# Roll layer by two images: VectorE's step reordered, the residual added by TensorE and moved by ScalarE; attention's output bias added in the embedding

## The chip, the cores and the metric

The kernel runs on one core of a Trainium2 chip. The metric is the device time of one execution in microseconds (us); lower is better. All data is float32.

## The reference, cut to what matters

32 images of 36 patches and 32 text tokens each give 68 tokens per image, 2176 tokens of 256 features, in 17 tiles of 128 tokens.

```
h = concat(patchify(x) @ W.T + b, txt)            # (32, 68, 256)
h = h + attention(layernorm(h))                   # windowed, 16 heads; ends in  out @ Wo + bo
h = h + ffn0(layernorm(h))                        # 64 experts, 8 per token, plus a shared one
h = h + roll(layernorm(h))
h = h + ffn1(layernorm(h))                        # 8 experts, 1 per token

roll(x):                                          # per image, S = 68, H = 16 heads of 16
  z = softmax((x @ W_A.T) * 16**-0.5, axis=tokens)            # (S, H)
  v = (x @ W_V.T).reshape(S, H, 16)
  out[i, h] = sum over j of  (z rolled by i, lower triangle)[h, i, j] * v[j, h]
  return out @ W_O.T + b_O
```

The kernel computes the rolled sum as a product of Fourier transforms over the tokens: transform v and z (real and imaginary part), multiply, transform back.

## The kernel before, in words

The stages follow each other with a barrier between them: `embed_and_norm` (L176), attention (`window_attention`, L342), the first mixture of experts, `roll_layer` (L1469), the second mixture. `h` is the residual stream [128, 17 tiles, 256] in SBUF, `xn` its normalised rows, `xT` these transposed.

**Embedding.** Four batches of eight images. TensorE sums the patches to columns and transposes them to tiles; VectorE copies a tile to `h`, takes its statistics, and normalises it to `xn` (L338); TensorE transposes `xn` back and ScalarE moves it to `xT` (L252). The batches have 4, 4, 4 and 5 tiles. SP loads patches, text and constants, then the attention weights wq, wk, wv and the biases bq, bk, bv, bo in this order, all on one semaphore, `attn_in`; attention waits for all seven (112).

**Attention.** Eight blocks of four images, eight steps in each. VectorE's step adds the mask (L566), takes the peak (L570) and normalises the step three before (L549, L553); in block 0 it also adds `bo` to two tiles of `h` per step (L545), and the seventeenth tile's add follows after the last block. POOL subtracts the peak (L425). The attention's own output is added to `h` in a later stage.

**Roll layer.** Sixteen groups of two images (136 tokens), in a software pipeline of 19 steps. In step i, group g1 = i-1 is on the way in, g2 = i-2 is multiplied, inverted and projected, and g3 = i-3 goes out; the order on each engine is written out by hand. On the way in, a tile of `h` gets its eight expert rows added (`combine`, L1854; POOL gathers them at L1571 into a ring of four tiles), is measured (L1861, L1862), its rstd is made on ScalarE (`root`, a logarithm and an exponential, L1763 and L1766), `scale` makes the shift on VectorE (L1869), ScalarE normalises (L1772), TensorE turns it (`turn`, L1583) and ScalarE moves it (L1778). Then come `mix_logits` (L1591: z in PSUM, moved by ScalarE at L1751), `values` (L1601, moved at L1758), and the softmax of z over the 68 tokens on [16, 2, 68]: `mix_shift` on VectorE (maximum L1874, subtraction L1875), `exp` on ScalarE (L1787), `mix_norm` on VectorE (sum L1880, reciprocal L1881, product L1882). `turn_mix` (L1616) and `forward_mix` (L1622) transform z, ScalarE moves both results (L1791, L1798). In the next step, `forward` transforms v, one product for the real part and one for the imaginary part (L1610), `multiply` makes four terms on VectorE (L1901), `invert` transforms back in 64 products (L1635), ScalarE moves the result (`move_out`, L1744), and `project` multiplies by W_O into `pr`, with b_O added by a product with the identity (L1645, L1647). One step later VectorE adds `pr` to `h` (`add_projected`, L1889), the tile is measured, normalised and turned a second time ("out"), and `choose` (L1668) makes the router logits of the last layer. SP writes the normalised tile and `h` to DRAM.

On VectorE a step is in this order before: scale in, add_projected, measure out, four multiplies, scale out, mix_shift, combine 0 to 3, mix_norm, combine 4 to 7, measure in. On TensorE: forward (both parts), turn in, mix_logits, values, turn out, invert, turn_mix, project, choose, forward_mix. On ScalarE: root in, normalise in, move turned in, root out, normalise out, move_mix, move_values, move turned out, exp, move_out, move_mix_turned, move_mix_forwarded. Steps 1, 2 and 16 have additional products without use on TensorE (`fill_logits`, `fill_values`).

Of the kernel before, what the change touches and what calls it, by code (L numbers as in the profile page):

```python
# [5 lines left out]
P = 128  # L6
D = 256
# [4 lines left out]
S = NPATCH + NTXT  # L12
# [163 lines left out]
def embed_and_norm(nc, a, k):  # L176
# [6 lines left out]
    with ExitStack() as st:  # L183
# [11 lines left out]
        (consts_in, bias_in, attn_in, txt_in, sums, moved, txt_placed, turned, placed, stated, measured, eps_set, rooted, inverted,  # L195
         normed, turned_back, turn_moved) = sems(
            nc, k, "emb", "consts_in bias_in attn_in txt_in sums moved txt_placed turned placed stated measured eps_set rooted inverted "
# [9 lines left out]
        with nc.Block() as block:  # L207

            @block.sync
            def _(sp):  # L210
# [109 lines left out]
            def _(dve):  # L320
                for i in range(NB):
# [15 lines left out]
                    for t in range(lo, hi):  # L337
                        nc.vector.tensor_scalar(xn[:, t, :], h[:, t, :], mv[:, t, 0:1], rstd[:, t:t + 1],  # L338
                                                ALU.subtract, ALU.mult).then_inc(normed, 1)


def window_attention(nc, a, k, m, aT, wo):  # L342
# [18 lines left out]
    with ExitStack() as st:  # L361
        sb = lambda n, s, d=fp32: k["sb"](f"wa_{n}", s, d, st)
        wq, wk, wv, bq, bk, bv, bo = (k["attn"][n] for n in ("wq", "wk", "wv", "bq", "bk", "bv", "bo"))
# [18 lines left out]
         peaked, shifted, exped, turn_moved, inverted, normalised, biased, ones_all) = sems(  # L382
            nc, k, "wa", "block_copied keys_spread vals_set scored masked turned weighted jobs_done "
            "jobs_moved placed peaked shifted exped turn_moved inverted normalised biased ones_all")
# [22 lines left out]
        with nc.Block() as block:  # L407
# [10 lines left out]
            def _(pool):  # L418
                nc.gpsimd.tensor_copy(xb[:, :, :], xT[:, :, 0:CB]).then_inc(block_copied, 1)
                head_of = k["const"]("head_of").unsqueeze(2).broadcast_to([P, PER, S])  # L420
                pool.wait_ge(w_in, 112)
# [35 lines left out]
            def _(pe):  # L457
# [6 lines left out]
                pe.wait_ge(w_in, 112)  # L464
# [78 lines left out]
            def _(dve):  # L543
                def add_bias(t):
                    nc.vector.tensor_tensor(h[:, t, :], h[:, t, :], bo[:, :], ALU.add).then_inc(biased, 1)  # L545

# [9 lines left out]
                def body(blk, table):  # L556
                    start = isinstance(blk, int) and blk == 0
                    for step in range(UNITS):
# [24 lines left out]
                add_bias(NT - 1)  # L583
# [4 lines left out]
            def _(act):  # L588
# [38 lines left out]
                act.wait_ge(w_in, 112)  # L627
# [841 lines left out]
def roll_layer(nc, a, k, r, wt, y_rows, shared_up, shared_down):  # L1469
# [30 lines left out]
    with ExitStack() as st:  # L1500
# [7 lines left out]
        zpeak, zsum = sb("zpeak", [H, GI]), sb("zsum", [H, GI])  # L1508
# [14 lines left out]
         z_shifted, exped, z_normed, z_turned, zt_moved, zf_done, zf_moved, v_done, v_moved, forwarded, terms,  # L1523
# [835 lines left out]
```

## Time and profile before

| what | value |
|---|---|
| three runs | 1069.63, 1071.5, 1072.02 us; median 1071.5 |
| profiled execution | 1072.1 us, its span 1070.3 us |
| mean granted TensorE clock of the span | 0.938 |
| busy over the span | TensorE 928.9 us (87%), VectorE 591.7 (55%), POOL 523.0 (49%), ScalarE 420.7 (39%) |
| roll layer | about 635 to 870 us of the span |
| steady steps of the roll layer | one is 758.12 to 769.13 us of the span |

The span goes from the first to the last instruction of one profiled execution. Shares are means over stages that have different limits, so a stage is read in the timeline of its own stretch. Names such as PE, DVE, ACT, POOL and SP are TensorE, VectorE, ScalarE, GpSimd and SyncE; L1882 is line 1882 of the kernel.

### The profile page before, as it was taken

What the parts mean: (1) busy time and instruction counts of PE and PEld (TensorE: products, weight loads), DVE (VectorE), ACT (ScalarE), POOL (GpSimd) and SP (SyncE); (2) the same over time, 40 slices, a digit from 0 to 9 for tenths busy, and PEclk for the clock granted to TensorE, in tenths of its full rate; (3) what the DMA queues carried; (4) which work ended last, traced back from release to release, by engine and by line L of the source; (5) the groups of instructions that cost most, each with busy time, mean ns of one, the idle gap of its engine ahead of it and who ended that gap; (6) DMA issues with size and microseconds to landing.
All of it is one profiled execution on the core that took longest, in us unless ns stands there. A gap on an engine that the chain in (4) does not pass through costs nothing. (4 is left out here: it accounts for less than half of the span.)

```text
span 1070.3 us, 29582 instructions
## 1 busy us (share of the span) xinstructions
PE 928.9 (87%) x10270; PEld 740.1 (69%) x10270; DVE 591.7 (55%) x1502; ACT 420.7 (39%) x1158; POOL 523.0 (49%) x714
## 2 busy tenths in 40 slices
PE   8689999987824999999999987889888945999996
PEld 6557777766823888888888876455555535888895
DVE  1678888866896677533333425687877551111111
ACT  2346676742424343343434421243433312332331
POOL 0055655620502777777677717777773002333332
PEclk9889999979968999999999999898998986999998
DMA  7010000002002988977788833354482046476650
GB/s 254 14 32 2 0 0 0 1 2 76 10 0 83 321 261 263 295 230 221 251 267 254 236 93 96 104 130 123 123 289 71 21 172 223 141 262 216 262 155 25
DMA packets 79820, 149.27 MB, mean 139 GB/s; under 512 B 18892, under 2 KB 53327, under 8 KB 75760
## 3 DMA queue, kind: packets, MB, share of 16 engines
q1 hardware_dynamic: 34768, 77.15, 21.4%
q0 software_dynamic: 17712, 47.88, 16.0%
q10 hardware_dynamic: 27248, 23.09, 6.4%
q8 instruction: 49, 0.80, 0.3%
q14 instruction: 43, 0.35, 0.1%
HBM read 200.22 MB, written 31.73 MB: 217 GB/s over the span
## 5 line engine op out<-in xcount | busy, mean ns | idle before, releaser
L1309 POOL DMA_INDIRECT x_x<-m_x_rows,x_idx x170 | 165.8, 975 | 74.6 <-issue 35.5
L1335 PE MATMUL x_pup<-x_xt,x_w 128*128 128x128 f32 (+1 forms) x2176 | 183.9, 251 | 0.0
L1335 PEld LDWEIGHTS x_pup<-x_xt,x_w 128*128 128x128 f32 (+1 forms) x2176 | 167.9, 165 | 5.8 <-issue 5.7
L1571 POOL DMA_INDIRECT rl_y<-m_y_rows,rl_idx x136 | 133.7, 983 | 45.6 <-issue 36.9
L1405 DVE TENSOR_TENSOR x_hid<-x_gate,x_pup 128x128 f32<-128x128 f32 x170 | 49.0, 288 | 148.0 <-ACT x_gate L1377 141.3
L1349 PE MATMUL x_pdown<-x_w,x_hid 128*128 128x256 f32 (+1 forms) x408 | 104.2, 389 | 0.2 <-DVE x_y L1412 0.2
L1373 ACT ACTIVATE x_xt<-x_pturn 128x256 f32<-128x256 f32 x170 | 65.2, 383 | 89.0 <-PE x_pturn L1320 86.1
L425 POOL TENSOR_TENSOR wa_probs<-wa_probs,wa_peak 68x544 f32<-68x544 f32 x64 | 70.8, 1106 | 59.5 <-DVE wa_peak L570 59.5
L2295 DVE TENSOR_TENSOR x_y<-x_pdown,x_b 128x256 f32<-128x256 f32 x21 | 8.9, 425 | 153.4 <-PE x_pdown L2251 153.4
L2281 ACT ACTIVATE x_hid<-x_pup,x_b 128x128 f32<-128x128 f32 (+1 forms) x200 | 52.7, 355 | 96.0 <-PE x_pup L2234 95.8
L1377 ACT ACTIVATE x_gate<-x_pup 128x128 f32<-128x128 f32 x170 | 47.1, 277 | 92.8 <-PE x_pup L1335 92.1
L1320 PE MATMUL x_pturn<-cst,x_x 128*128 128x128 f32 x340 | 68.0, 282 | 9.6 <-DMA x_x<-m_x_rows,x_idx 9.6
L1412 DVE COPY x_y<-x_pdown 128x256 f32<-128x256 f32 x170 | 71.3, 420 | 2.0 <-PE x_pdown L1349 0.5
L1320 PEld LDWEIGHTS x_pturn<-cst,x_x 128*128 128x128 f32 x340 | 45.3, 142 | 37.1 <-issue 13.1
L1854 DVE SCALAR_TENSOR_TENSOR h<-rl_y,m_wt,h 128x256 f32<-128x256 f32 x136 | 65.8, 484 | 3.8
L2190 POOL DMA_INDIRECT out_h<-x_y,m_ids_out x21 | 21.2, 1007 | 93.5 <-DVE x_y L2298 87.3
L618 ACT ACTIVATE wa_probs<-wa_probs 68x544 f32<-68x544 f32 x64 | 42.1, 658 | 51.7 <-POOL wa_probs L425 51.6
L1294 POOL COPY x_idx<-m_ids 128x1 uint32 (+1 forms) x170 | 37.2, 219 | 41.5 <-POOLq L902 40.5
L2234 PE MATMUL x_pup<-x_xt,late_w 128*128 128x128 f32 x384 | 48.2, 287 | 3.7 <-ACT x_xt L2271 1.9
L2234 PEld LDWEIGHTS x_pup<-x_xt,late_w 128*128 128x128 f32 x384 | 47.1, 202 | 6.2 <-issue 3.7
L1349 PEld LDWEIGHTS x_pdown<-x_w,x_hid 128*128 128x128 f32 (+1 forms) x408 | 48.1, 173 | 3.9 <-DVE x_hid L1405 0.6
L566 DVE TENSOR_TENSOR wa_probs<-wa_scores,cst 68x544 f32<-68x544 f32 x64 | 46.0, 718 | 8.1 <-PE wa_scores L521 5.8
(327 smaller groups left out, 1895.0 us busy)
## 6 DMA issues: line engine op xcount, KB each, us to landing
x_w<-in_experts SPq DMA_DIRECT2D x204, 384.0 KB
late_w<-in_w SPq DMA_DIRECT2D x28, 1024.0 KB, 12.3
m_y_rows<-x_y ACTq DMA_DIRECT2D x170, 128.0 KB
xT<-in_w SPq DMA_DIRECT2D x12, 1024.0 KB, 6.2
xn<-in_w SPq DMA_DIRECT2D x10, 1024.0 KB, 10.5
h<-in_w SPq DMA_DIRECT2D x10, 1024.0 KB, 14.6
m_x_rows<-xn SPq DMA_DIRECT2D x34, 128.0 KB, 1.8
x_x<-m_x_rows,x_idx POOLq DMA_INDIRECT x170, 4.7
```

Of the source, the lines that this page charges most:

```text
L425: nc.gpsimd.tensor_tensor(probs[:, slot4, :, :], probs[:, slot4, :, :], peak[:, slot2, :].unsqueeze(2).broadcast_to([S, HC, S]), ALU.subtr ...
L1309: nc.gpsimd.indirect_dma_start(x[:, s, :], None, x_rows, bass.IndirectOffsetOnAxis(ap=idx[:, s:s + 1], axis=0))\
L1320: mm = nc.tensor.transpose(pturn[:, bank, c * P:(c + 1) * P], x[:, s, c * P:(c + 1) * P], ident)
L1335: mm = nc.tensor.matmul(pup[rows:rows + wide, bank, m * P + side * wide:m * P + (side + 1) * wide], w[:, lane, first:first + wide], xt[:, ...
L1349: mm = nc.tensor.matmul(pdown[rows, s % 2, 0:D], hid[:, s, rows], w[:, lane, UP:W], start=True, stop=True)
L1373: nc.scalar.activation(xt[:, s, :], pturn[:, bank, 0:D], ACT.Copy).then_inc(turn_moved, 1)
L1405: nc.vector.tensor_tensor(hid[:, s, :], gate[:, s, :], pup[:, bank, P:2 * P], ALU.mult)\
L1412: nc.vector.tensor_copy(y[:, s, :], pdown[:, s % 2, 0:D]).then_inc(down_moved, 1)
L1571: nc.gpsimd.indirect_dma_start(y[:, t % YR, kk, :], None, y_rows, bass.IndirectOffsetOnAxis(ap=idx[:, n:n + 1], axis=0))\
L1854: nc.vector.scalar_tensor_tensor(h[:, t, :], y[:, t % YR, kk, :], wt[:, t, kk:kk + 1], h[:, t, :], ALU.mult, ALU.add).then_inc(added, 1)
L2234: mm = nc.tensor.matmul(pup[rows:rows + wide, s, half, to:to + wide], w1[l][:, c, first:first + wide], xt[:, s, at:at + wide], start=(c == ...
L2281: ins = nc.scalar.activation(hid[:, s, f, side * wide:(side + 1) * wide], pup[:, s, f // HB, at:at + wide], ACT.Gelu, bias=b1[:, l, f:f + 1])
```

## The change

Attention's output bias: `bo` gets a semaphore of its own (`bo_in`) and is loaded first among the attention weights; VectorE adds it to `h` in `embed_and_norm`, after each batch's normalise for the batch before, and for the last batch behind it. The adds of attention's block 0 are gone.

Roll layer: (1) `project` adds the residual tile by a product of the identity with `h`, ScalarE moves the sum from PSUM to `h` (`move_projected`), and `add_projected` is gone. (2) z is negated as it is moved, VectorE takes one minimum (`mix_least`), and ScalarE's exponential takes it as a bias with scale -1, one instruction for each image, which also gives the sum; the subtraction and the sum on VectorE are gone. (3) The order on the three engines is another one, and `forward` and `multiply` are split into their two parts.

```diff
@@ embed_and_norm, SP
+                sp.dma_start(attn["bo"][:, :], a["bo"].broadcast_to([P, D])).then_inc(bo_in, 16)
                 for name in ("wq", "wk", "wv"):
...
-                sp.dma_start(attn["bo"][:, :], a["bo"].broadcast_to([P, D])).then_inc(attn_in, 16)
@@ embed_and_norm, VectorE
+                def add_bias(i):
+                    dve.wait_ge(bo_in, 16)
+                    dve.wait_ge(normed, BATCHES[i][1])
+                    for t in range(*BATCHES[i]):
+                        nc.vector.tensor_tensor(h[:, t, :], h[:, t, :], attn["bo"][:, :], ALU.add).then_inc(residual_biased, 1)
...
+                    if i:
+                        add_bias(i - 1)
+                add_bias(NB - 1)
@@ window_attention, VectorE
-                        if start:
-                            for t in range(2 * step, 2 * step + 2):
-                                add_bias(t)
...
-                add_bias(NT - 1)
@@ roll_layer, TensorE
                         nc.tensor.matmul(pr[:, s, :], ident, late["b_o"][:, :], start=True, stop=False)
+                        nc.tensor.matmul(pr[:, s, :], ident, h[:, t, :], start=False, stop=False)
...
                     if has2:
-                        forward(g2, 0)
                         forward(g2, 1)
...
+                    if has2:
                         invert(g2)
+                    if has2 and not has1:
...
                     for t in outs:
                         turn("out", t)
...
-                    if has2 and has1:
-                        invert(g2)
                     if has1:
                         turn_mix(g1)
                     if has2 and has1:
                         project(g2)
-                    for t in outs:
-                        choose(t)
...
                     if has1:
                         forward_mix(g1)
+                        forward(g1, 0)
+                    for t in outs:
+                        choose(t)
@@ roll_layer, ScalarE
+                def move_projected(g):
+                    ts = tiles_out(g)
+                    act.wait_ge(projected, g + 1)
+                    nc.scalar.activation(h[:, ts[0]:ts[-1] + 1, :], pr[:, 0:len(ts), :], ACT.Copy).then_inc(proj_added, 1)
...
-                                         scale=float(HD) ** -0.5).then_inc(z_moved, 1)
+                                         scale=-float(HD) ** -0.5).then_inc(z_moved, 1)
...
-                    nc.scalar.activation(z[:, :, :], z[:, :, :], ACT.Exp).then_inc(exped, 1)
+                    act.wait_ge(least_found, g + 1)
+                    for b in range(GI):
+                        ins = nc.scalar.activation(z[:, b, :], z[:, b, :], ACT.Exp, bias=zleast[:, b:b + 1], scale=-1.0,
+                                                   accum_out=zsum[:, b:b + 1])
+                    ins.then_inc(exped, 1)
...
+                    if has1:
+                        move_mix(g1)
...
                     if outs:
                         root("out", outs)
+                    if has1:
+                        move_values(g1)
+                    if outs:
                         normalise("out", outs)
...
                         exp(g1)
                     if has2 and has1:
                         move_out(g2)
+                    for t in outs:
+                        move_turned("out", t)
                     if has1:
                         move_mix_turned(g1)
+                    if has2:
+                        move_projected(g2)
+                    if has1:
                         move_mix_forwarded(g1)
@@ roll_layer, VectorE
+                    nc.vector.tensor_reduce(zleast[:, :], z[:, :, :], AX.X, ALU.min).then_inc(least_found, 1)
...
-                    link(nc.vector.tensor_reduce(zsum[:, :], z[:, :, :], AX.X, ALU.add))
...
+                    if has2:
+                        multiply(g2, 0)
                     if has1:
                         scale("in", tiles_in(g1))
-                    if has2 and not has1:
-                        multiply(g2)
+                    if has2:
+                        multiply(g2, 1)
                     if outs:
-                        add_projected(g3)
                         dve.wait_ge(proj_added, g3 + 1)
                     for t in outs:
                         measure("out", t)
-                    if has2 and has1:
-                        multiply(g2)
-                    if outs:
-                        scale("out", outs)
...
-                    if has1:
-                        mix_shift(g1)
                     if now:
                         combine(now[-1], 0, K0 // 2)
+                    if outs:
+                        scale("out", outs)
+                    if has1:
+                        mix_least(g1)
+                    if now:
+                        combine(now[-1], K0 // 2, K0 - 2)
                     if has1:
                         mix_norm(g1)
                     if now:
-                        combine(now[-1], K0 // 2, K0)
+                        combine(now[-1], K0 - 2, K0)
                         measure("in", now[-1])
```

## Rows read from the trace of the kernel before

**Rows 1.** The page's costliest groups (count | busy, mean ns | idle before, releaser): gathers.

```profile
L1571 POOL DMA_INDIRECT rl_y<-m_y_rows,rl_idx x136 | 133.7, 983 | 45.6 <-issue 36.9 <-PE rl_pf L1678 6.3 <-DVE h L1854 1.2
```

**Rows 2.** Windows: stretch, us; PE, PEld, DVE, ACT, POOL busy; PEclk; DMA share; GB/s.

```profile
733.20:733.60 0.40, 0.40 (x3) 0.33 (x2) 0.38 (x1) 0.00 (x0) 0.31 (x1) 0.70 0.46 133
```

**Rows 3.** Timeline (start, us, what, idle before and releaser): three turns of the mix.

```profile
732.71 0.24 PE L1616 MATMUL rl_pz<-cst,rl_z 16*68 16x16 f32 x2 [0.97 <-DVE rl_z L1882]
...
791.14 0.24 PE L1616 MATMUL rl_pz<-cst,rl_z 16*68 16x16 f32 x2 [1.00 <-DVE rl_z L1882]
...
840.09 0.24 PE L1616 MATMUL rl_pz<-cst,rl_z 16*68 16x16 f32 x2 [0.97 <-DVE rl_z L1882]
```

**Rows 4.** Timeline of TensorE, one step of the roll layer.

```profile
758.12 0.24 PE L1616 MATMUL rl_pz<-cst,rl_z 16*68 16x16 f32 x2 [0.96 <-DVE rl_z L1882]
758.29 0.70 PE L1645 MATMUL rl_pr<-late_b_o,cst 128*128 128x256 f32 x2
...
759.69 0.51 PE L1668 MATMUL rl_po<-late_wr,rl_x 128*128 128x8 f32 x4
760.05 0.41 PE L1622 MATMUL rl_pz<-rl_zt,cst 68*68 68x32 f32 x4
760.30 1.91 PE L1610 MATMUL rl_pf<-rl_v,cst 68*68 68x512 f32 x4
...
763.06 0.64 PE L1591 MATMUL rl_pz<-xT,late_w_a 128*16 128x136 f32 x4 [0.47 <-ACT xT L1778]
763.62 1.94 PE L1601 MATMUL rl_pv<-late_w_v,xT 128*68 128x256 f32 x8
765.64 0.44 PE L1583 MATMUL rl_pt<-cst,xn 128*128 128x128 f32 x2
766.01 2.12 PE L1635 MATMUL rl_po<-cst,rl_term 68*64 68x68 f32 x64
769.13 0.24 PE L1616 MATMUL rl_pz<-cst,rl_z 16*68 16x16 f32 x2 [1.00 <-DVE rl_z L1882]
```

**Rows 5.** Timeline of VectorE in the same step.

```profile
761.30 0.16 DVE L1869 SCALAR_TENSOR_TENSOR rl_shift<-rl_mv,rl_rstd 128x1 f32<-128x1 f32 x1 [0.60 <-ACT rl_rstd L1766]
...
762.40 2.48 DVE L1901 TENSOR_TENSOR rl_term<-rl_pf,rl_zf 68x512 f32<-68x512 f32 x4
...
765.78 0.28 DVE L1874 TENSOR_REDUCE rl_zpeak<-rl_z 16x2 f32<-16x136 f32 x1 [0.83 <-ACT rl_z L1751]
```

**Rows 6.** Timeline of ScalarE in the same step.

```profile
764.99 0.60 ACT L1772 ACTIVATE xn<-h,rl_shift,rl_rstd 128x256 f32<-128x256 f32 x1 [1.57 <-DVE rl_shift L1869]
...
765.66 0.59 ACT L1758 ACTIVATE rl_v<-rl_pv 68x512 f32<-68x512 f32 x1
...
766.42 0.32 ACT L1787 ACTIVATE rl_z<-rl_z 16x136 f32<-16x136 f32 x1
```

**Rows 7.** Timeline of VectorE: the first mask add of attention's blocks 0 to 3.

```profile
57.83 0.72 DVE L566 TENSOR_TENSOR wa_probs<-wa_scores,cst 68x544 f32<-68x544 f32 x1 [4.33 <-PE wa_scores L521]
...
82.80 0.71 DVE L566 TENSOR_TENSOR wa_probs<-wa_scores,cst 68x544 f32<-68x544 f32 x1
...
102.87 0.72 DVE L566 TENSOR_TENSOR wa_probs<-wa_scores,cst 68x544 f32<-68x544 f32 x1 [0.49 <-POOL wa_probs L425]
...
123.44 0.72 DVE L566 TENSOR_TENSOR wa_probs<-wa_scores,cst 68x544 f32<-68x544 f32 x1 [0.44 <-POOL wa_probs L425]
```

**Rows 8.** Timeline of VectorE and ScalarE: embedding's end and two pairs of bias adds.

```profile
42.67 0.85 DVE L326 COPY h<-emb_pt 128x256 f32<-128x256 f32 x2 [1.44 <-PE emb_pt L295]
...
47.23 1.71 DVE L338 TENSOR_SCALAR xn<-h,n_mv,n_rstd 128x256 f32<-128x256 f32 x5
...
48.43 2.09 ACT L252 ACTIVATE xT<-emb_pn 128x256 f32<-128x256 f32 x5 [1.52 <-PE emb_pn L305]
...
59.22 0.75 DVE L545 TENSOR_TENSOR h<-h,late_b 128x256 f32<-128x256 f32 x2
...
74.74 1.56 DVE L545 TENSOR_TENSOR h<-h,late_b 128x256 f32<-128x256 f32 x2
```

More of the change, by code:

```diff
@@ L194, in embed_and_norm @@
         pn = st.enter_context(nc.psum_tensor("emb_pn", [P, 3, 512], fp32))
-        (consts_in, bias_in, attn_in, txt_in, sums, moved, txt_placed, turned, placed, stated, measured, eps_set, rooted, inverted,
+        (consts_in, bias_in, attn_in, bo_in, residual_biased, txt_in, sums, moved, txt_placed, turned, placed, stated, measured, eps_set, rooted, inverted,
          normed, turned_back, turn_moved) = sems(
-            nc, k, "emb", "consts_in bias_in attn_in txt_in sums moved txt_placed turned placed stated measured eps_set rooted inverted "
+            nc, k, "emb", "consts_in bias_in attn_in bo_in residual_biased txt_in sums moved txt_placed turned placed stated measured eps_set rooted inverted "
             "normed turned_back turn_moved")
@@ L362, in window_attention @@
         sb = lambda n, s, d=fp32: k["sb"](f"wa_{n}", s, d, st)
-        wq, wk, wv, bq, bk, bv, bo = (k["attn"][n] for n in ("wq", "wk", "wv", "bq", "bk", "bv", "bo"))
+        wq, wk, wv, bq, bk, bv = (k["attn"][n] for n in ("wq", "wk", "wv", "bq", "bk", "bv"))
         w_in = k["attn_in"]
@@ L381, in window_attention @@
         (block_copied, keys_spread, vals_set, scored, masked, turned, weighted, jobs_done, jobs_moved, placed,
-         peaked, shifted, exped, turn_moved, inverted, normalised, biased, ones_all) = sems(
+         peaked, shifted, exped, turn_moved, inverted, normalised, ones_all) = sems(
             nc, k, "wa", "block_copied keys_spread vals_set scored masked turned weighted jobs_done "
-            "jobs_moved placed peaked shifted exped turn_moved inverted normalised biased ones_all")
+            "jobs_moved placed peaked shifted exped turn_moved inverted normalised ones_all")
         def four(ap):
@@ L420, in _ @@
                 head_of = k["const"]("head_of").unsqueeze(2).broadcast_to([P, PER, S])
-                pool.wait_ge(w_in, 112)
+                pool.wait_ge(w_in, 96)
                 def shift(unit, slot4, slot2):
@@ L462, in project @@
                     mm.then_inc(jobs_done, 1)
-                pe.wait_ge(w_in, 112)
+                pe.wait_ge(w_in, 96)
                 project(wq, 0, lambda c: xT[:, c, 0:CB])
@@ L543, in _ @@
             def _(dve):
-                def add_bias(t):
-                    nc.vector.tensor_tensor(h[:, t, :], h[:, t, :], bo[:, :], ALU.add).then_inc(biased, 1)
                 def normalise(unit, slot, early=False):
@@ L625, in move_turned @@
                                          ACT.Copy).then_inc(turn_moved, 1)
-                act.wait_ge(w_in, 112)
+                act.wait_ge(w_in, 96)
                 act.wait_ge(jobs_done, 1)
@@ L1507, in roll_layer @@
         z = sb("z", [H, GI, S])
-        zpeak, zsum = sb("zpeak", [H, GI]), sb("zsum", [H, GI])
+        zleast, zsum = sb("zleast", [H, GI]), sb("zsum", [H, GI])
         zt = sb("zt", [S, GI, H])
@@ L1822, in _ @@
                         root("out", outs)
+                    if has1:
+                        move_values(g1)
+                    if outs:
                         normalise("out", outs)
-                    if has1:
-                        move_mix(g1)
-                        move_values(g1)
-                    for t in outs:
-                        move_turned("out", t)
                     if has1:
@@ L1870, in scale, with mix_least @@
                                                    ALU.mult, ALU.mult).then_inc(scaled, 1)
-                def mix_shift(g):
+                def mix_least(g):
                     dve.wait_ge(z_moved, g + 1)
-                    link(nc.vector.tensor_reduce(zpeak[:, :], z[:, :, :], AX.X, ALU.max))
-                    nc.vector.tensor_tensor(z[:, :, :], z[:, :, :], zpeak[:, :].unsqueeze(2).broadcast_to([H, GI, S]),
-                                            ALU.subtract).then_inc(z_shifted, 1)
+                    if g:
+                        dve.wait_ge(z_normed, g)
+                    nc.vector.tensor_reduce(zleast[:, :], z[:, :, :], AX.X, ALU.min).then_inc(least_found, 1)
                 def mix_norm(g):
                     dve.wait_ge(exped, g + 1)
-                    link(nc.vector.tensor_reduce(zsum[:, :], z[:, :, :], AX.X, ALU.add))
                     link(nc.vector.reciprocal(zsum[:, :], zsum[:, :]))
@@ L1883, in mix_norm, with multiply @@
                                             ALU.mult).then_inc(z_normed, 1)
-                def add_projected(g):
-                    ts = tiles_out(g)
-                    dve.wait_ge(projected, g + 1)
-                    dve.wait_ge(normed, turn_at["in", ts[-1]] + 1)
-                    nc.vector.tensor_tensor(h[:, ts[0]:ts[-1] + 1, :], h[:, ts[0]:ts[-1] + 1, :], pr[:, 0:len(ts), :],
-                                            ALU.add).then_inc(proj_added, 1)
-                def multiply(g):
+                def multiply(g, part):
                     s = g % 2
@@ L1896, in multiply @@
                         dve.wait_ge(inverted, g - 1)
-                    for i, part, zpart in ((0, 0, 0), (2, 0, 1), (1, 1, 1), (3, 1, 0)):
+                    for i, zpart in (((0, 0), (2, 1)) if part == 0 else ((1, 1), (3, 0))):
                         n = g * 2 + part
```

6 lines of the change are left out of this document (2 added, 4 removed).

## The prediction, made before the changed kernel ran

> **What bounds the kernel now.** I read the page's costliest groups first, to see where each part of the change lies and whether a queue could already be the limit. The roll layer's row gathers are the longest POOL group: 136 of 0.983 us, with 36.9 us of issue idle over the 121 that have any, so about 0.30 us between two [rows 1]. Eight per tile are 8 x (0.983 + 0.30) = 10.3 us, a little less than a step of the roll layer. This queue is a floor, not the present bound.
>
> The steady step comes next, in the timeline of one step at full clock, one engine after the other. From one turn of the mix to the next it is 769.13 - 758.12 = 11.01 us [rows 4]; 15 of these steps matter. The reader is to see three waits. TensorE stands 1.00 us behind the inversion until VectorE has normalised z, and 0.47 us until ScalarE has moved the turned tile [rows 4]. VectorE itself stands 0.60 us for rstd and 0.83 us for z [rows 5]. z comes late because ScalarE normalises the outgoing tile ahead of it, and that one waited 1.57 us for a VectorE scale queued behind four multiplies [rows 6]. So the loop now goes through VectorE's order, and ScalarE lies in it twice. TensorE's own work is 11.01 - 1.00 - 0.47 = 9.54 us.
>
> Then the clock. The window just behind one turn of the mix shows a granted clock of 0.70, part of it at 1.2 GHz in place of 2.4 [rows 2]; I count three such falls in the layer, at 733, 791 and 815 us, each 0.2 to 0.7 us after a turn of the mix that had stood 0.97 to 1.00 us behind the inversion. Their price comes from distances between turns [rows 3]. 732.71 to 791.14 is 58.43 us for 5 steps (55.05), so 3.4 lost. 791.14 to 840.09 is 48.95 for 4 steps (44.04), so 4.9 lost on two falls. Together 8.3 us.
>
> Last, attention: its first block of four images takes 82.80 - 57.83 = 24.97 us, the next two 20.07 and 20.57 [rows 7]. Only the first carries the bias adds.
>
> **The change part by part.** *Bias out of attention.* Sixteen adds leave VectorE in block 0; a pair was 0.75 us alone and 1.56 us beside POOL's work [rows 8]. The block can save nothing at least (its scores may come late anyway: the first mask add waited 4.33 us for them [rows 7]) and 24.97 - 20.07 = 4.9 us at most. I take its distance to block 2, 4.4, less 0.5 because block 1 runs 0.5 faster than block 2, a catch-up that a faster block 0 ends: **-3.9**. The seventeenth add follows the blocks and I cost it at nothing.
>
> *Bias into the embedding.* Eight adds, two batches of four, run in VectorE's waits for the transposes. The narrowest wait that I use is 1.44 us [rows 8], against 4 x 0.375 = 1.5, so 0.06 could stick out; where that cover fails they cost up to 1.5 each batch. The remaining nine come after the last normalise: 47.23 + 1.71 = 48.94 us is where VectorE ends now, + 9 x 0.375 = 52.3, against ScalarE's present end at 48.43 + 2.09 = 50.52 [rows 8]. The embedding's end moves by **+1.8**. At the price beside POOL (0.78 each) it would be 55.96, +5.4; at best the next stage's own first wait (4.33 us) hides it and it is 0. POOL has nothing to do there, so I take the short price. The bias is issued three matrices earlier on SP, ahead of what attention waits for, but attention waited for the same seven transfers before, in sum the same bytes; nothing.
>
> *The roll step.* VectorE loses the residual add, a subtract and a reduction and gets its order changed: scale-in stands behind two multiplies instead of ahead, scale-out and the z work behind four combines. TensorE gains one 128x256 product per tile and now transforms the next group's first part at the step's end; ScalarE gains a move of the projected tile and a second exponential. I follow the new loop from a turn of the mix. Where an operation's row is cut by the next start, I use the starts.
> 1. Turn of the mix to projection: 758.29 - 758.12 = 0.17.
> 2. Projection: 759.69 - 758.29 = 1.40 for three products, 0.43 to 0.53 each; the residual is a fourth: + 0.45 = 1.85.
> 3. Transform of the mix: 760.30 - 760.05 = 0.25.
> 4. First forward transform until VectorE can multiply: 1.91 / 2 = 0.96, + 762.40 - 762.21 = 0.19 of hand-over, less overlap; 1.05 to 1.19, taken 1.12.
> 5. Two multiplies: 2.48 / 2 = 1.24.
> 6. Scale-in to the end of the next tile's turn and its move, where the z logits start: 763.06 - 761.30 = 1.76.
> 7. z logits 763.62 - 763.06 = 0.56, values 1.94 less 0.08 of overlap = 1.86, inversion 2.12 - 0.06 = 2.06, outgoing turn 766.01 - 765.64 = 0.37.
>
> Steps 1 to 4 and 7 are from [rows 4], 5 and 6 from [rows 5], with 6 ending in [rows 4]. Sum: 0.17 + 1.85 + 0.25 + 1.12 + 1.24 + 1.76 + 0.56 + 1.86 + 2.06 + 0.37 = 11.24 us, with ends 11.05 and 11.35. Against 11.01 that is +0.23, times 15 **+3.4** (+0.6 to +5.1). VectorE's own work shrinks, but the step does not: the loop now goes TensorE, VectorE's first multiplies, ScalarE's normalise, TensorE. The other chains have slack. From the first multiply's start, z's minimum is reached at 5.4 (both multiply pairs, scale, measure, four combines). ScalarE gets to the exponential only after moving the values (0.59) and normalising the outgoing tile (0.60): values end at 1.24 + 1.76 + 0.56 + 1.94 = 5.5, so about 6.7. Two at 0.32 each [rows 6] end near 7.3, VectorE's normalising near 7.85; the inversion and outgoing turn let TensorE arrive at 7.85. That cover is thin, 0 to 0.2 us, and is a rival below. The move of the projection runs beside the forward transform and costs nothing; should it not, up to 0.6 us a step come on top (the values' move, twice its size, took 0.59 [rows 6]). The second exponential as such is bounded by 0 (hidden) and 0.64 (a full one, and as much again to read out sums): I take 0.
>
> A rule speaks against this. The exponential of 136 columns took 0.32 us [rows 6]. The Trainium skill, "ScalarE: Activation LUTs", section "What ACT_TABLE_LOAD costs", gives 186 ns + 0.833 ns a column for a plain activation and 280 ns + 0.833 for one whose bias is a pointer, with 93 ns of overlap: 0.30 for the old one, which the row agrees with, and 0.58 for two of 68 columns, an estimate. If that stood on the path it would be +0.26 x 15 = +3.9; by the rows it lies under the inversion.
>
> *The clock.* In the new order the inversion is followed by the outgoing turn and the mix at once, so the place where all three falls came has no idle time left. New idle stands elsewhere: about 1.05 us ahead of the incoming turn and 0.5 ahead of the z logits. I expect the three falls gone, **-8.3**, and one short one in their place, **+1.5** (between 0 and as much as the old ones).
>
> **The sum.** 1072.1 - 3.9 + 1.8 + 3.4 - 8.3 + 1.5 = 1066.6 us, made against the profiled execution, 1072.1 us with a span of 1070.3. That execution is 0.6 above the median of the runs, 1071.5, so I give **1066**.
>
> **The rivals.** *A: the falls only move.* As many come at the new idle time as left the old one: -3.9 + 1.8 + 3.4 = +1.3, **1073**. For it: over 1 us of idle remains in each step. Against: the fall followed one place, the inversion's small products with idle behind, three times of three.
> *B, slower: the new idle brings more falls than the old.* Place: the 1.05 us ahead of the incoming turn, followed by short transposes and 0.5 us more. Price: 3.4 us each as the first of the old. Four give -3.9 + 1.8 + 3.4 + 13.6 = +14.9 less the old 8.3: +6.6, **1078**. It decides from the third fall on: (8.3 - 1.3) / 3.4 = 2.1. For it: idle now stands in two pieces close together. Against: 0.47 of it stood there before without a fall [rows 4].
> *C: the exponentials end last.* With up to 0.64 a step beyond cover, 15 x 0.64 = +9.6 on my 1066, **1076** at the full price, 1071 at half. For it: the cover of 0 to 0.2 us. Against: the old one ends at 766.42 + 0.32 = 766.74, 1.4 us ahead of the inversion's end [rows 4, 6].
> *D: the loop's waits close* and the step falls to TensorE's own work, 9.54 + 0.43 = 9.97; the gathers' 10.3 do not bind while they run ahead. 15 x (9.97 - 11.01) = -15.6: 1071.5 - 2.1 - 15.6 - 8.3 = **1046**. Against: it needs steps 4 to 6 hidden, and the order offers TensorE nothing to do there.
>
> **How the numbers follow.** Forecast 0.44 (its own range 1061 to 1070), A 0.22, B 0.16, C 0.10, D 0.08. The range leaves out D and the tail of B: 1058 to 1078. About 0.2%, 2.1 us, is what runs of this kernel can tell from no change. Faster: 0.40 of the forecast, 0.06 of A and D's 0.08, 0.54. Same: 0.04 + 0.10 + 0.02 of C, 0.16. Slower: 0.06 of A, B's 0.16, 0.08 of C, 0.30.
>
> **What would show it.** Block 0 of attention within 0.5 us of 21; the embedding's last VectorE add near 52.3. In the roll layer a step of 11.05 to 11.35 at full clock, the turn of the mix with no wait for z's normalising, the residual product at 0.43 to 0.53, and some 1 us of TensorE idle ahead of the incoming turn. A wait of the mix's turn on VectorE shows C; a step under 10.3 D; falls of the clock ahead of the z logits A or B. The forecast is wrong if the clock falls in this layer cost more than 4 us, or the step leaves its bounds.

## The result: slower, 1077.6 us, and the profile after

Three runs of the changed kernel took 1077.57, 1077.48 and 1079.47 us, median 1077.57, against 1071.5 before; the ratio is 1.0066, with a 95% interval of 1.0041 to 1.0092. Ratios here and below compare means, without one run of after_add that was over 1.5% slower than the fastest run of that kernel. That is 6 us slower where 5.5 us faster was forecast, and close to what rival B gave (1078). The profiled execution has a span of 1075.8 us against 1070.3, +5.5.

Where the span's difference arises is read by laying equal instructions of both traces beside each other, difference after less before: first mask add of attention +1.07; the same add of block 2 -2.50; second reciprocal of the next stage's layernorm (for four tiles) -1.63, after -3.32 at the first (two tiles); first turn of the mix -1.24 (676.04 against 677.28); last turn of the mix +4.95 (856.96 against 852.01); end +5.5. So attention gained, a part of it was lost directly behind, and the roll layer lost 6.2 us: its fifteen distances between turns sum to 174.73 us before and 180.92 after. These are the first and the last turn of the mix in TensorE's timeline, before and then after:

```profile
677.28 0.24 PE L1616 MATMUL rl_pz<-cst,rl_z 16*68 16x16 f32 x2
...
852.01 0.24 PE L1616 MATMUL rl_pz<-cst,rl_z 16*68 16x16 f32 x2
```

```profile
676.04 0.24 PE L1618 MATMUL rl_pz<-cst,rl_z 16*68 16x16 f32 x2
...
856.96 0.24 PE L1618 MATMUL rl_pz<-cst,rl_z 16*68 16x16 f32 x2
```

First one step of the changed roll layer, at full clock. This is TensorE's timeline (start, us, what, idle before and its releaser), to be laid beside [rows 4]:

```profile
711.01 0.24 PE L1618 MATMUL rl_pz<-cst,rl_z 16*68 16x16 f32 x2
711.19 0.70 PE L1647 MATMUL rl_pr<-late_b_o,cst 128*128 128x256 f32 x2
711.72 0.59 PE L1648 MATMUL rl_pr<-h,cst 128*128 128x256 f32 x2
712.15 1.03 PE L1650 MATMUL rl_pr<-late_w_o,xT 128*128 128x256 f32 x4
713.02 0.38 PE L1624 MATMUL rl_pz<-rl_zt,cst 68*68 68x32 f32 x4
713.23 1.05 PE L1612 MATMUL rl_pf<-rl_v,cst 68*68 68x512 f32 x2
...
716.46 0.44 PE L1585 MATMUL rl_pt<-cst,xn 128*128 128x128 f32 x2 [0.92 <-ACT xn L1780]
717.38 0.64 PE L1593 MATMUL rl_pz<-xT,late_w_a 128*16 128x136 f32 x4 [0.47 <-ACT xT L1786]
717.94 1.94 PE L1603 MATMUL rl_pv<-late_w_v,xT 128*68 128x256 f32 x8
719.82 2.12 PE L1637 MATMUL rl_po<-cst,rl_term 68*64 68x68 f32 x64
721.87 0.44 PE L1585 MATMUL rl_pt<-cst,xn 128*128 128x128 f32 x2
722.29 0.24 PE L1618 MATMUL rl_pz<-cst,rl_z 16*68 16x16 f32 x2
```

The reader is to see that the step is 722.29 - 711.01 = 11.28 us, that the turn of the mix waits for nothing any more, and that TensorE's 1.00 us behind the inversion has become 0.92 us ahead of the incoming turn, with 0.47 us shortly behind it. Now the next step, with a fall of the clock, in the same view:

```profile
728.66 0.70 PE L1593 MATMUL rl_pz<-xT,late_w_a 128*16 128x136 f32 x4 [0.47 <-ACT xT L1786]
729.29 3.52 PE L1603 MATMUL rl_pv<-late_w_v,xT 128*68 128x256 f32 x8
732.74 2.12 PE L1637 MATMUL rl_po<-cst,rl_term 68*64 68x68 f32 x64
...
735.22 0.24 PE L1618 MATMUL rl_pz<-cst,rl_z 16*68 16x16 f32 x2
```

The eight products of the values take 3.52 us in place of 1.94, and the step 735.22 - 722.29 = 12.93. The windows view (stretch, us, busy PE, PEld, DVE, ACT, POOL, PEclk, DMA share, GB/s) shows the clock of such a fall, the first of the layer's steady part, and the mean over most of the layer:

```profile
705.20:705.60 0.40, 0.40 (x2) 0.23 (x2) 0.38 (x1) 0.40 (x2) 0.40 (x1) 0.52 0.41 92
...
690.00:840.00 150.00, 131.50 (x1230) 83.91 (x1229) 98.89 (x259) 62.09 (x218) 93.13 (x96) 0.92 0.47 135
```

From 705.2 to about 708.6 us the products run at 1.2 GHz in place of 2.4. There are seven such falls, at 705, 729, 753, 767, 791, 814 and 828 us, all in the z logits or the values, and the steps that hold them take 12.85 to 12.96 us; the others 11.26 to 11.31. The mean clock over the stretch, 0.92, is also the one before:

```profile
690.00:840.00 150.00, 131.76 (x1293) 84.95 (x1291) 116.68 (x307) 56.64 (x181) 95.15 (x97) 0.92 0.47 137
```

The mean alone hides what a fall costs. Before, the fall at 733 us held the clock at 0.50 for 10.2 us (the windows, and the turn of the mix at that step's end):

```profile
733.40:743.60 10.20, 9.73 (x27) 5.17 (x26) 6.77 (x18) 2.78 (x9) 7.76 (x9) 0.50 0.41 122
```

```profile
746.88 0.24 PE L1616 MATMUL rl_pz<-cst,rl_z 16*68 16x16 f32 x2
```

It cost 3.4 us (two steps of 14.17 and 11.24 against 11.01), since the wait of 1.0 us behind the inversion was gone at the end of that step: the turn of the mix at 746.88 waits for nothing. After, each fall lasts 3.4 us, lies over z logits and values, where TensorE has no wait left to give, and costs 12.9 - 11.28 = 1.6 us.

The embedding and attention, VectorE's timeline of the changed kernel, beside [rows 7, 8]:

```profile
46.84 1.70 DVE L344 TENSOR_SCALAR xn<-h,n_mv,n_rstd 128x256 f32<-128x256 f32 x5
48.46 3.11 DVE L325 TENSOR_TENSOR h<-h,late_b 128x256 f32<-128x256 f32 x9
...
58.90 0.72 DVE L572 TENSOR_TENSOR wa_probs<-wa_scores,cst 68x544 f32<-68x544 f32 x1 [4.33 <-PE wa_scores L530]
...
79.57 0.72 DVE L572 TENSOR_TENSOR wa_probs<-wa_scores,cst 68x544 f32<-68x544 f32 x1 [0.18 <-POOL wa_probs L434]
...
100.37 0.72 DVE L572 TENSOR_TENSOR wa_probs<-wa_scores,cst 68x544 f32<-68x544 f32 x1 [0.48 <-POOL wa_probs L434]
```

Block 0 now takes 79.57 - 58.90 = 20.67 us, block 1 20.80. The nine adds end at 48.46 + 3.11 = 51.57. The gathers' group is as it was (136 of 0.977 us, 0.983 before [rows 1]), and in the step from 711.01 on no combine waits for one.

### The profile page after: what moved, and what is told of

The parts are those of the page before. It is cut to its first block and busy times, and to the rows that moved or that the text cites. A ratio compares the mean times of both kernels' runs of the same rounds, so it can differ in the third digit from the quotient of the medians.

```text
span 1075.8 us, 29701 instructions
## 1 busy us (share of the span) xinstructions
PE 939.6 (87%) x10304; PEld 747.3 (69%) x10304; DVE 571.1 (53%) x1454; ACT 434.2 (40%) x1222; POOL 519.3 (48%) x714
## 5 line engine op out<-in xcount | busy, mean ns | idle before, releaser
L1909 DVE TENSOR_TENSOR rl_term<-rl_pf,rl_zf 68x512 f32<-68x512 f32 x64 | 40.8, 679 | 33.2 <-PE rl_pf L1612 33.2
## 6 DMA issues: line engine op xcount, KB each, us to landing
xn<-in_w SPq DMA_DIRECT2D x10, 1024.0 KB, 11.4
```

## The experiments

Theory 1: the bias part gains about 2.5 us; the roll layer loses 0.27 us a step at full clock (4 us), and falls of the clock, brought by TensorE's idle time ahead of the incoming turn, cost 11.3 us in place of 8.3. Rival 2: TensorE's added work brings the falls. Rival 3: another chain (the exponentials, VectorE, ScalarE) sets the step. Each kernel was timed beside the kernel before on its chip, which took 1072.0 to 1072.9 us there. Sums of the fifteen distances between the first and last turn of the mix are called the layer's length; before it is 174.73 us, after 180.92.

**The parts alone.** *bias_only* is the kernel before with the bias part of the change, *roll_only* with the roll part; their edits are the hunks shown above.

> The kernel before with only the bias part of the change (bo loaded first, added in the embedding, gone from attention). Theory 1 (the bias part is a small gain, the roll layer holds the whole loss): attention's first block falls from 24.97 to about 20.7 us, the embedding ends about 1.1 us later, the second block is 0.7 longer, in sum -2.5; the roll layer keeps its step of 11.01 and its three clock falls; 1068 to 1070.5 us, 1 to 3 below before. Rival (the bias part costs what it saves, because clock behind attention changes): 1071 to 1073 us.

Measured: 1070.12 us, ratio 0.9981 (0.9965 to 0.9996), as theory 1 expected. The first mask add came at 58.81, that of block 2 at 100.17. But the roll layer, which is the code of before, had five falls in this execution where the kernel before had three, and a length of 178.10. So the number of falls is not a property of the code alone; single runs lay between 1068.0 and 1075.47 us.

> The kernel before with only the roll layer's part of the change. Theory 1: step 11.28 at full clock against 11.01 (+4) and about seven short clock falls of 1.6 us in place of three that cost 8.3 (+3): 1078 to 1081 us, 7 to 9 above before. Rival (the loss comes from the bias part shifting the layer against some other clock or queue): 1071 to 1075 us.

Measured: 1081.37 us, ratio 1.0079 (1.0063 to 1.0095); the layer's length is 180.93 us, as in the changed kernel, with seven falls again. The loss lies in the roll part, wherever the layer starts.

**The idle time filled.** *after_fill* gives TensorE products without use in the two idle places in every step, *before_fill* behind the inversion.

```diff
@@ after_fill, against the changed kernel
-                    if g1 in FILLED:
+                    if has1:
                         fill_logits(g1, 4)
                     for t in tiles_in(g1):
                         turn("in", t)
-                    if g1 in FILLED:
+                    if has1:
                         fill_logits(g1, 1)
@@ before_fill, against the kernel before
                     if has2 and has1:
                         invert(g2)
+                        if g1 not in FILLED:
+                            fill_values(g1, 4)
```

> The changed kernel with products without use (4 of 512 columns ahead of the incoming turn, 1 ahead of the z logits) in every step of the roll layer, not only in steps 1, 2 and 16. Theory 1 (the falls come from TensorE's two idle stretches there): none or one fall left between 700 and 840 us, step at full clock 11.28 to 11.4, 1066 to 1069 us. Rival 2 (the falls come from TensorE's added work, a residual product per tile): as many falls as in the changed kernel or more, 1077 to 1085 us. Rival 3 (the fillers delay the incoming turn): step 11.5 or more, 1070 to 1075.

> The kernel before with four products without use (512 columns each) behind the inversion in every steady step of the roll layer, where TensorE stood 1.00 us. Theory 1: the three falls at 733, 791 and 815 us are gone, step 11.01, 1062.5 to 1065 us, 7 to 9 below before. Rival 2 (more work brings more falls): three or more falls, 1071 to 1080 us. Rival 3 (the fillers delay the mix's turn): step 11.2 or more, 1066 to 1070 us.

Measured: after_fill 1064.34 us, ratio 0.9926 (0.9912 to 0.994); before_fill 1063.04 us, ratio 0.9909 (0.9892 to 0.9926). Neither has a fall between 690 and 840 us. (The first is faster than the 1066 to 1069 us expected.) after_fill's timeline of TensorE and, below it, its windows:

```profile
713.25 0.81 PE L1658 MATMUL rl_pz<-m_chosen_b,m_before_b 128*128 128x512 bf16 x3
714.12 0.44 PE L1585 MATMUL rl_pt<-cst,xn 128*128 128x128 f32 x2
714.39 0.38 PE L1658 MATMUL rl_pz<-m_chosen_b,m_before_b 128*128 128x512 bf16 x1
715.03 0.64 PE L1593 MATMUL rl_pz<-xT,late_w_a 128*16 128x136 f32 x4 [0.26 <-ACT xT L1786]
```

```profile
690.00:840.00 150.00, 144.49 (x1392) 92.38 (x1404) 106.63 (x280) 67.39 (x238) 93.00 (x96) 1.00 0.47 136
```

The fillers sit in the wait (the incoming turn at 714.12 comes 5.45 us after the turn of the mix at 708.67; in the changed kernel 716.46 - 711.01 = 5.45), the step stays 11.28, and the clock 1.00. The first and last turn of the mix, in after_fill and then in before_fill:

```profile
675.30 0.24 PE L1618 MATMUL rl_pz<-cst,rl_z 16*68 16x16 f32 x2
...
844.80 0.24 PE L1618 MATMUL rl_pz<-cst,rl_z 16*68 16x16 f32 x2
```

```profile
679.14 0.24 PE L1616 MATMUL rl_pz<-cst,rl_z 16*68 16x16 f32 x2
...
845.60 0.24 PE L1616 MATMUL rl_pz<-cst,rl_z 16*68 16x16 f32 x2
```

The layer's length falls from 180.92 to 169.50, so the falls cost 11.4 us after; before_fill's is 166.46 against 174.73, so 8.3 before. Against the same 166.46, the old order's five falls in bias_only's trace cost 178.10 - 166.46 = 11.6: the 8.3 is one execution's figure. The spans fall by more than the lengths (14.8 and 9.9 us): the part behind the last turn of the mix, whose code is the same, is shorter too (by 2.6 and 3.5 us), which was not followed up. Rival 2 falls: both kernels have more work on TensorE, and no falls.

**Which idle place.** *after_fill_in* fills only ahead of the incoming turn (the first of after_fill's two edits), *after_fill_z* only ahead of the z logits (the second).

> The changed kernel with products without use only ahead of the incoming turn (4 in every step), the 0.47 us ahead of the z logits left idle. If the longer idle stretch decides: no falls or one, as in after_fill, 1063 to 1067 us. If both stretches together are needed: three or more falls, 1069 to 1075 us.

> The changed kernel with one product without use ahead of the z logits in every step, so the 0.47 us there shrink to some 0.26 and the 0.92 us ahead of the incoming turn stay idle. If the long idle stretch alone brings the falls: seven as in the changed kernel, 1076 to 1080 us. If the two stretches together do: two falls or none, 1065 to 1069 us.

Measured: after_fill_in 1064.48 us, ratio 0.9923 (0.9906 to 0.9941), no fall in the steady steps, length 169.63. after_fill_z 1072.65 us, ratio 1.0004 (0.9985 to 1.0023): six falls, in every second step, 1.3 to 1.6 us each, length 178.33. The falls stay as in the first expectation, the time lies between the two; 2.6 of the 5 us against the changed kernel lie in the layer, the rest was not traced further. The 0.92 us stretch is the one that matters most: filled, no fall is left; with only the other one filled, six are, where the changed kernel had seven. The 0.47 us alone, as in after_fill_in and in before_fill, brought none there, and one in bias_fill below.

**Less work on TensorE.** *after_add* leaves the residual on VectorE in the new order; *after_add_fill* is that with after_fill's edits.

```diff
-                        nc.tensor.matmul(pr[:, s, :], ident, h[:, t, :], start=False, stop=False)
...
-                    if has2:
-                        move_projected(g2)
...
                     if outs:
+                        add_projected(g3)
                         dve.wait_ge(proj_added, g3 + 1)
```

> The changed kernel with the residual back on VectorE (add_projected ahead of measure out, no residual product, no move by ScalarE), all else as changed. Theory 1 (the residual product stands on the loop with its 0.43 us; the falls come from idle, which stays): step at full clock 10.85 in place of 11.28, seven falls or more, 1069 to 1073 us. Rival 2 (TensorE's added work brings the falls): step 10.85 and three falls or fewer, 1060 to 1066 us. Rival 3 (VectorE or ScalarE's exponentials hold the step): step above 11.1, 1074 to 1078.

> The kernel of after_add with the products without use of after_fill (4 ahead of the incoming turn, 1 ahead of the z logits, every step). Theory 1: step 10.85, no falls, 1057 to 1060 us (after_fill's 1064.3 less 15 x 0.43). Rival 3 (another chain ends at about 11.1 or later): 1061 to 1065 us.

Measured: after_add 1088.3 us, ratio 1.0107 (1.0066 to 1.0148), single runs 1074.74 to 1089.57; after_add_fill 1057.43, ratio 0.9855 (0.9836 to 0.9875). The step at full clock is 10.85 in after_add and 10.84 to 10.85 in every steady step of after_add_fill, 0.43 less than 11.28, as expected. But in after_add the clock falls in every step from 716 us on, from 727 us on for about 6.8 us each time, and such a step takes 13.65. Its waits of TensorE (waited for, us in total, times, longest) and windows:

```profile
PE rl_pt L1585 <- ACT xn L1774: 11.4, 12, 1.3
PE rl_pz L1593 <- ACT xT L1780: 5.7, 12, 0.5
```

```profile
690.00:840.00 150.00, 132.90 (x1110) 81.27 (x1110) 97.19 (x256) 54.65 (x192) 93.89 (x97) 0.78 0.46 134
```

A clock of 0.78 with less work asked of TensorE is rival 2's opposite. All three times expected for after_add missed (the highest was 1078), the one for after_add_fill held. The mechanism of theory 1 held; its time reckoned with far too little of the clock's cost.

**The softmax.** *after_fill_max* is after_fill with the old softmax (maximum and subtraction on VectorE, one exponential, sum on VectorE); this is ScalarE's part of the edit.

```diff
-                    for b in range(GI):
-                        ins = nc.scalar.activation(z[:, b, :], z[:, b, :], ACT.Exp, bias=zleast[:, b:b + 1], scale=-1.0,
-                                                   accum_out=zsum[:, b:b + 1])
+                    nc.scalar.activation(z[:, :, :], z[:, :, :], ACT.Exp)
```

> after_fill with the old softmax in the new order (maximum and subtraction on VectorE, one exponential of 136 columns, sum on VectorE). Theory 1 (the softmax does not set the step, the inversion and the outgoing turn do): step 11.28 again, 1063 to 1066 us. Rival (the two exponentials with their sums read out end last by a few tenths): step 11.0 to 11.15, 1060 to 1062 us. Other side (VectorE's three extra operations end last): step 11.4 or more, 1066 us or more.

Measured: 1063.39 us, ratio 0.9913 (0.9882 to 0.9944); step 11.25 against 11.28. The exponentials do not set the step here (rival C). In the changed kernel they look like this, ScalarE's timeline and then VectorE's:

```profile
720.97 0.33 ACT L1796 ACTIVATE rl_z<-rl_z,rl_zleast 16x68 f32<-16x68 f32 x1
721.21 0.18 ACT L1796 ACTIVATION_READ_ACCUMULATOR rl_z<-rl_z,rl_zleast 16x1 f32 x1
721.30 0.34 ACT L1796 ACTIVATE rl_z<-rl_z,rl_zleast 16x68 f32<-16x68 f32 x1
721.54 0.19 ACT L1796 ACTIVATION_READ_ACCUMULATOR rl_z<-rl_z,rl_zleast 16x1 f32 x1
```

```profile
721.76 0.15 DVE L1896 RECIPROCAL rl_zsum<-rl_zsum 16x2 f32<-16x2 f32 x1 [1.10 <-ACT rl_z L1796]
721.95 0.29 DVE L1897 TENSOR_TENSOR rl_z<-rl_z,rl_zsum 16x136 f32<-16x136 f32 x1
```

z is normal at 722.24, the turn of the mix starts at 722.29: the cover was as thin as the prediction said, and held.

**The bias part without the clock's chance.** *bias_fill* is bias_only with before_fill's edit.

> The kernel of before_fill with the bias part of the change. Theory 1: the bias part's gain in attention without the clock's chance behind it, 2.0 to 2.5 below before_fill: 1060 to 1061.5 us. Rival (the gain is given back behind attention): 1062.5 to 1063.5 us.

Measured: 1061.1 us, ratio 0.9894 (0.9874 to 0.9915), against before_fill's 0.9909: 1.9 us less between the two medians, on two chips and with intervals that overlap. Its trace has one fall in the layer, at 802 us, at the start of the z logits, behind the 0.47 us that were not filled; that step took 12.25. The sign agrees; the size is not settled by these runs.

**A shorter loop.** If the step is the sum along the loop, the projection need not stand in it. *loop_cut* is after_add with this order, *loop_cut_fill* the same with three products without use.

```diff
                     if has1:
                         turn_mix(g1)
-                    if has2 and has1:
-                        project(g2)
...
                         forward_mix(g1)
                         forward(g1, 0)
-                    for t in outs:
-                        choose(t)
+                    if has2 and has1:
+                        project(g2)
@@ ahead of mix_logits
+                    for t in tiles_out(g3 - 1):
+                        choose(t)
@@ ScalarE
+                    if has1:
+                        move_mix_turned(g1)
                     for t in outs:
                         move_turned("out", t)
@@ loop_cut_fill only
+                    if has1 and g1 not in FILLED:
+                        fill_values(g1, 2)
                     if has1:
                         turn_mix(g1)
+                    if has1 and g1 not in FILLED:
+                        fill_values(g1, 1)
```

> The kernel of after_add (residual on VectorE, no fillers) with the projection behind the next group's first forward transform and the router product ahead of the z logits; ScalarE moves the mix's first transform ahead of the outgoing tile. Theory 1 (the step is the sum along the loop, so the projection's 1.40 us leave it and about 0.4 us of wait for ScalarE's move come in): step 9.8 to 10.0 at full clock, idle in three pieces of at most 0.5 us, few falls, 1043 to 1050 us. Rival 2 (falls stay as in after_add, one each step): step 12 or more, 1070 to 1085 us. Rival 3 (VectorE or the gathers end last): step 10.2 to 10.5, 1050 to 1056 us.

> The kernel of loop_cut with three products without use in each steady step, two ahead of the mix's turn (idle 0.43 us there) and one behind it (0.28). Theory 1 (what remains of loop_cut's loss is the clock falls): no falls between 700 and 840 us, step 10.3 to 10.45, 14 steps of 0.4 to 0.55 less than after_add_fill's 10.85: 1050 to 1053 us. Rival (the falls need other idle, or the fillers delay the turn): falls in three or more steps or a step of 10.6 or more, 1054 to 1060 us.

Measured: loop_cut 1056.7 us, ratio 0.984 (0.9812 to 0.9868), single runs 1053.44 to 1065.41; loop_cut_fill 1049.03 us, ratio 0.9783 (0.9759 to 0.9807), the fastest of all, and faster than both kernels. Both lie about 1 us outside the nearest time expected (1056 and 1050). loop_cut_fill's step is 10.29 to 10.32 with no fall of the clock; one step at 770 us took 11.14. In loop_cut the clock fell in six steps of the traced execution. A full-clock step of loop_cut, TensorE's timeline, then ScalarE's and VectorE's:

```profile
806.39 0.24 PE L1618 MATMUL rl_pz<-cst,rl_z 16*68 16x16 f32 x2 [0.43 <-DVE rl_z L1891]
...
815.82 0.44 PE L1585 MATMUL rl_pt<-cst,xn 128*128 128x128 f32 x2
816.68 0.24 PE L1618 MATMUL rl_pz<-cst,rl_z 16*68 16x16 f32 x2 [0.43 <-DVE rl_z L1891]
```

```profile
814.85 0.60 ACT L1776 ACTIVATE xn<-h,rl_shift,rl_rstd 128x256 f32<-128x256 f32 x1 [0.33 <-DVE rl_shift L1879]
815.36 0.34 ACT L1792 ACTIVATE rl_z<-rl_z,rl_zleast 16x68 f32<-16x68 f32 x1
...
815.93 0.18 ACT L1792 ACTIVATION_READ_ACCUMULATOR rl_z<-rl_z,rl_zleast 16x1 f32 x1
```

```profile
814.66 0.15 DVE L1879 SCALAR_TENSOR_TENSOR rl_shift<-rl_mv,rl_rstd 128x1 f32<-128x1 f32 x1
...
816.34 0.29 DVE L1891 TENSOR_TENSOR rl_z<-rl_z,rl_zsum 16x136 f32<-16x136 f32 x1
```

10.30 is more than the 9.8 to 10.0 of theory 1 and lies in rival 3's step: the projection left the loop, and by this trace a chain that had been hidden ends last. The outgoing scale at 814.66 (behind the combines) releases ScalarE's normalise, which stands ahead of the exponentials, and z's normalising ends 0.43 us after TensorE could have turned it. No run shortens that chain, so this is a reading and not a test.

The gathers, which by the prediction's reckoning also take 10.3 us a tile, do not set this step: loop_cut's last one ends at 813.07, and the two steps from 816.68 on still take 10.30 and 10.29. They are close, though. In loop_cut_fill's step of 11.14 us, VectorE's timeline has a combine that waits for one:

```profile
779.48 1.00 DVE L1868 SCALAR_TENSOR_TENSOR h<-rl_y,m_wt,h 128x256 f32<-128x256 f32 x2 [1.07 <-DMA rl_y<-m_y_rows,rl_idx]
```

## Why the prediction was wrong, point by point

**The clock: the step that failed.** The prediction expected "the three falls gone, -8.3, and one short one in their place, +1.5", -6.8 in sum. The runs show seven falls that cost 11.4 us where the old ones cost 8.3, +3.1. The 8.3 varies from one execution to another (11.6 in bias_only), but the medians of several runs agree: filling took 9.9 us off the kernel before, 9.0 off bias_only (to bias_fill) and 13.2 off the changed kernel, 3 to 4 us more, while the kernel before differs by 1.4 us between chips. The first half was right: no fall begins behind the inversion any more. The second was not: the idle time, moved ahead of the incoming turn, brings falls too, and more of them (after_fill_in removes all, after_fill_z leaves six). I had tied the falls to one place, the inversion's small products with idle time behind, because all three came there; but a stretch of about 1 us of idle time and one of 0.47 are in a step of either order, and I gave the cases in which they matter, A and B, only 0.38 together. Rival B names the place right; its price per fall was too high (3.4 against 1.6) and its count too low (four against seven), and the two errors cancelled. The difference between -6.8 and +3.1, 9.9 us, is most of the 11.6 us between 1066 and 1077.6.

**The roll step: right.** Forecast 11.24 us with ends 11.05 and 11.35, measured 11.28. By the terms, in the timeline after: projection 1.83 (1.85 forecast), with the residual product at 0.43; first transform to the multiply 1.19 (1.12; VectorE's multiply started at 714.42); z logits 0.56, values 1.88 (1.86), inversion 2.05 (2.06), outgoing turn 0.42 (0.37). From the multiply's start to the z logits it is 717.38 - 714.42 = 2.96 (1.24 + 1.76 = 3.00 forecast). Over the fifteen distances the step's part is +3.0 where +3.4 was forecast: without falls they sum to 169.50 (after_fill) against 166.46 (before_fill). It is less than 15 x 0.27, since the first distance became shorter (10.41 against 11.16). These 3.0 and the falls' 3.1 are the layer's 6.2 us. That the projection stands in a loop is shown by after_add (0.43 less, as the one product) and by loop_cut (0.55 less again, up to the next chain).

**The exponentials, rival C: right that they were hidden,** by 0.05 us in the trace; after_fill_max shows 0.03 a step. With their sums read out the two take 0.76 us (720.97 to 721.73), 0.44 more than the old one's 0.32 and within the bound of 0.64 that the prediction set for it.

**Attention and the embedding: right in sign and near in size.** Block 0 saved 4.30 (3.9 forecast, with block 1's loss in it; block 1 lost 0.73, 0.5 forecast), so 3.57. The embedding's part is +1.07 at the first mask add (+1.8 forecast), because the last normalise ended 0.4 us earlier (46.84 + 1.70 = 48.54 against 48.94) and the adds stand 0.35 us apart, not 0.375. In sum -2.50 against -2.1. One reading was wrong without harm to the sum: the pair of adds taken as alone [rows 8] had POOL's subtraction (L425) beside it from 59.38 us, which took 1.54 us there and 1.09 at 67.22. There the adds' price seems to have fallen on POOL.

**What was not foreseen** is the stretch behind attention: the clock falls there at 241 us in the changed kernel and not before, 240 to 250 us in the windows of the one and of the other:

```profile
240.00:250.00 10.00, 9.27 (x47) 7.77 (x48) 4.89 (x19) 2.17 (x7) 0.00 (x0) 0.83 0.23 78
```

```profile
240.00:250.00 10.00, 7.60 (x45) 5.93 (x44) 7.24 (x27) 3.35 (x7) 0.00 (x0) 1.00 0.17 55
```

Between the two reciprocals above, 1.7 of 3.3 us are given back. It need not be the bias part's doing: roll_only, whose attention is that of before, has the same clock in that window (0.83), and bias_fill, which has the bias part, has 1.00. No experiment was made on it.

**Open.** Why the falls are three to five in the old order, about one in two steps in the changed one and nearly every step in after_add was not settled. The idle time alone does not order them: 0.97 to 1.00 + 0.47 of 11.01 us before, 0.92 + 0.47 of 11.28 after, 0.92 + 0.47 of 10.85 in after_add. The two stretches lie 5.1 us apart before (762.59 + 0.47 to 768.13 [rows 4]) and 0.44 us apart after (one turn), which would fit more falls. Against it: after_fill_z, with the second stretch cut to 0.26 us, still has six. A kernel that changes only the distance was not run.

## What to carry to other kernels

When an order by hand is changed, list where TensorE's idle stretches go, not only whether the old ones vanish: here a move of 1 us of idle time from one place to another kept the falls of the clock, and a few products without use, put into the wait, took them away, but for one in bias_fill, at no cost to the step at either place (8.3 us off the layer in the old order, 11.4 in the new). Cost such a change first along the loop of dependences, term by term from the starts in the timeline, since this came out to 0.04 us; and treat the clock as a term of its own with a wide range. Work taken off the engine with the clock can make a kernel slower, as after_add did, until its idle time is filled.

## What the runs showed of the hardware that was not expected

- The granted clock in after_add fell to 0.78 over 150 us although TensorE had less to do than in the changed kernel (0.92), and single runs of it spread over 15 us (1074.74 to 1089.57); with the idle time filled, runs spread over 1 us (1057.23 to 1058.19).
- The same code showed three falls in the kernel before and five in bias_only, whose layer differs only in when it starts.
- An exponential that gives its sum is two instructions in the trace: 0.33 to 0.34 us for 68 columns and 0.18 to 0.19 us to read the accumulator. The Trainium skill, "ScalarE: Activation LUTs", section "What ACT_TABLE_LOAD costs", gives 280 ns + 0.833 ns a column for one with a bias by pointer, 0.34 for 68 columns, an estimate; the rows' 0.33 to 0.34 agree. The read comes behind it: from the first exponential's start to the end of the second read, 0.76 us.
